# Two graph layers on one core: score rows turned on chip, two softmax passes moved from VectorE to GpSimd

## What is computed

```python
h = relu(layernorm(x))
D = abs(h[:, :, None, :] - h[:, None, :, :])        # 64 x 128 x 128 x 128
t = leaky(batchnorm(einsum('bijc,oc->bijo', D, W1) + b1))   # 64 channels, statistics over b, i, j
s = where(adj > 0, einsum('bijo,uo->bij', t, W2) + b2, -9e15)
A = softmax(s, axis=-1)
y = leaky(batchnorm((A @ h) @ Wg.T + bg))
x = x + concat([h, y]) @ Wt.T + bt
```

## Time and profile before

| | us |
|---|---|
| median of 3 runs | 1188.4 |
| lowest and highest of them | 1184.73, 1188.98 |
| time of the profiled execution | 1189.32 |
| its span, first to last instruction | 1187.5 |
| PE busy | 1062.9 (90%) |
| DVE busy | 1058.1 (89%) |
| ACT busy | 994.8 (84%) |
| POOL busy | 541.3 (46%) |

### The profile page before, as it was taken

How to read it: one execution, slowest core, us unless ns; L and a number is a source line. 1 busy time by engine, 2 the same in 40 slices (tenths; PEclk the granted TensorE clock), 3 DMA queues, 4 the chain that set the end, 5 groups by cost and what they waited for, 6 DMA issues and landing times.

```text
span 1187.5 us, 17527 instructions
## 1 busy us (share of the span) xinstructions
PE 1062.9 (90%) x6376; PEld 463.2 (39%) x6376; DVE 1058.1 (89%) x1418; ACT 994.8 (84%) x1238; POOL 541.3 (46%) x251
## 2 busy tenths in 40 slices
PE   3889999999999999999999599999999999548997
PEld 1333333333333333333333212333333333338886
DVE  6899999999999999999999787999999999435787
ACT  3879999999999899999999599898988989006987
POOL 6466667666666666666667101111122211261331
PEclk9989999999999999999999799999999999758998
DMA  6324343434343334343434789999999998700222
GB/s 165 131 118 177 143 173 146 178 142 164 156 178 142 160 160 177 142 168 152 178 142 188 299 305 358 366 355 360 349 358 350 347 348 296 191 4 12 71 80 72
DMA packets 118005, 237.52 MB, mean 200 GB/s; under 512 B 17568, under 2 KB 65952, under 8 KB 117920
## 3 DMA queue, kind: packets, MB, share of 16 engines
q1 hardware_dynamic: 116336, 235.70, 54.6%
q10 hardware_dynamic: 1584, 0.69, 0.3%
HBM read 126.52 MB, written 109.84 MB: 199 GB/s over the span
## 4 chain that ended last, share of the span: by engine, by line
PE 45%; DVE 32%; ACT 9%; issue 7%; DMA 3%; POOL 2%; SPq 1%; POOLq 0%; DVEq 0%; ACTq 0%
PE psum L708 18%; DVE store L275 12%; PE psum L718 11%; PE psum L722 8%; DVE plain_st L979 4%; ACT store L610 3%; ACT store L556 3%; DVE store L1058 3%; DMA early<-score_rows 2%; PE psum L821 1%; PE psum L680 1%; PE psum L698 1%; PE psum L778 1%; PE psum L855 1%; POOL store L475 1%
## 5 line engine op out<-in xcount | busy, mean ns | idle before, releaser
L708 PE MATMUL psum<-store,w1tt_sb 128*64 128x512 f32 x1792 | 426.0, 605 | 37.4 <-ACT store L556 19.2
L275 POOL TENSOR_TENSOR store<-h_ext 128x2048 f32<-128x2048 f32 (+1 forms) x96 | 386.5, 4028 | 140.9 <-PE psum L708 137.0
L275 DVE TENSOR_TENSOR store<-psum,h_ext 128x2048 f32<-128x2048 f32 x160 | 364.0, 2275 | 0.9 <-ACT h_ext L526 0.9
L556 ACT ACTIVATE store<-store 128x2048 f32<-128x2048 f32 x160 | 305.1, 1929 | 15.2 <-DVE store L275 10.3
L708 PEld LDWEIGHTS psum<-store,w1tt_sb 128*64 128x64 f32 x1792 | 121.7, 137 | 277.5 <-issue 223.5
L610 ACT ACTIVATE store<-store,st 128x1024 f32<-128x1024 f32 x192 | 225.8, 1242 | 1.4 <-DVE st L1045 1.4
L718 PE MATMUL psum<-store,w_twice 128*64 128x512 f32 x768 | 201.5, 603 | 3.9 <-DVE early L944 3.5
L979 DVE BATCH_NORM_STATS2 plain_st<-store 128x6 f32<-128x512 f32 x256 | 160.6, 678 | 0.6 <-ACT store L568 0.6
L722 PE MATMUL psum<-early 128*64 128x512 bf16 x1152 | 158.0, 381 | 0.0
L275 DVE TENSOR_TENSOR store<-h_ext 128x2048 f32<-128x2048 f32 x64 | 139.1, 2173 | 2.6 <-PE psum L708 2.6
L778 PE MATMUL psum<-store,w_rows 128*32 128x512 f32 x1024 | 131.8, 606 | 5.4 <-ACT store L610 5.4
(11 more groups left out here) (153 smaller groups left out, 1143.4 us busy)
## 6 DMA issues: line engine op xcount, KB each, us to landing
kept_products<-store SPq DMA_DIRECT2D x192, 512.0 KB, 2.7
store<-kept_products SPq DMA_DIRECT2D x192, 512.0 KB, 7.5
early<-score_skew SPq DMA_DIRECT2D x16, 384.0 KB, 6.4
early<-adj SPq DMA_DIRECT2D x16, 256.0 KB, 8.0
early<-adj_t SPq DMA_DIRECT2D x16, 256.0 KB, 3.0
store<-x SPq DMA_DIRECT2D x16, 256.0 KB, 4.8
out<-early SPq DMA_DIRECT2D x16, 256.0 KB, 2.4
score_rows<-early SPq DMA_DIRECT2D x64, 32.0 KB, 3.7
```

What stands on the lines that cost most here:

```text
L275: return engine.tensor_tensor(t[:, :, 0:steps, :], nodes.unsqueeze(2).broadcast_to([C, 2, steps, N]), windows(h_ext[:, 2 * c, :], STEP * m ...
L556: nc.scalar.activation(t, t, ACT.Abs).then_inc(abs_ready, 1)
L708: last = nc.tensor.matmul(t[MID * g:MID * g + MID, b, :], w1tt_sb[:, 0:MID], diff[slot][:, g, b * BANK:b * BANK + BANK], start=True, stop= ...
```

## The change

It has these parts:

1. The round trip of the score rows through DRAM is gone (`store_rows`, `load_dist`, `s_dist`). `turn_dist` transposes `s_rows` straight from SBUF in four 128x128 pieces, and `take_turned` sorts the columns in four tensor_tensor instructions, one for each graph.
2. `att_sum` transposes the half matrix only (four PE transposes in place of eight matmuls). The half that isn't transposed is added to the mask on POOL (a second instruction in `sum_half`).
3. The subtraction of the maximum (`shift`) and the product with the reciprocal (`weight`) are POOL instructions. `mask(j + 1)` stands between them.
4. All 16 `x_and_bias` stand behind the last `weight`.
5. `again` computes the last chunk of a couple in full width (`repeats=True`), in one instruction in place of three.
6. All steps are set anew, and the tail has 63 steps in place of 72.

```diff
-        EVAC, DIST_T, TURN, SUM, SCORES, EXP, NORM, TURN_P, COPY, MIX, MIX_COPY, OUT, Y = \
-            19, 32, 33, 50, 52, 56, 58, 61, 62, 64, 65, 67, 69
-        STORE_ROWS, LOAD_DIST, STORE_SKEW, LOAD_HALF, LOAD_ADJ = 21, 26, 35, 41, 30
-        TAIL = 72
+            19, 21, 22, 40, 42, 46, 48, 51, 52, 54, 55, 58, 60
+        STORE_SKEW, LOAD_HALF, LOAD_ADJ = 24, 30, 22
+        TAIL = 63
...
-            if m == PER - 1:
+            if m == PER - 1 and not repeats:
...
             def load_half(j):
                 sp.wait_ge(skew_stored[j % 2], 16 * (j // 2 + 2))
                 if j > 0:
                     sp.wait_ge(s_sum, j)
+                    sp.wait_ge(half_masked, j)
...
                         if j == NQ - 1 and step != LOAD_ADJ:
-                            part = (STORE_ROWS, LOAD_DIST, STORE_SKEW, LOAD_HALF).index(step)
-                            for q in range(4 * part, 4 * part + 4):
+                            for q in range(6) if step == STORE_SKEW else range(6, NQ):
                                 load_x(q)
...
             def sum_half(j):
...
+                pool.wait_ge(half_summed, j + 1)
+                nc.gpsimd.tensor_tensor(mneg[:, :, :], mneg[:, :, :], s_half[:, :, 0:N], ALU.add).then_inc(half_masked, 1)
...
+            def shift(j):
+                pool.wait_ge(max_ready, j + 1)
+                nc.gpsimd.tensor_tensor(s_shift[:, :, :], s_shift[:, :, :], bcast(rows[:, 0, :], N), ALU.subtract)\
+                  .then_inc(s_shifted, 1)
+
+            def weight(j):
+                pool.wait_ge(weight_ready, j + 1)
+                nc.gpsimd.tensor_tensor(prob[:, :, :], prob[:, :, :], bcast(rows[:, 2, :], N), ALU.mult)\
+                  .then_inc(prob_ready, 1)
+
+            mask(0)
             for j in range(NQ):
-                mask(j)
-                if j == NQ - 1:
-                    pool.wait_ge(bt_ready, 1)
-                    for q in range(8):
-                        x_and_bias(q)
                 sum_half(j)
+                shift(j)
+                if j + 1 < NQ:
+                    mask(j + 1)
+                weight(j)
                 if 5 <= j < 5 + MRING:
                     mask_l1(j - 5)
-            for q in range(8, NQ):
+            pool.wait_ge(bt_ready, 1)
+            for q in range(NQ):
                 x_and_bias(q)
...
             def turn_dist(j):
-                pe.wait_ge(dist_in, 16 * (j + 1))
+                pe.wait_ge(rows_ready, j + 1)
                 at_one(QCH * j + DIST_T)
-                for b in range(QUAD):
-                    last = nc.tensor.transpose(att[1].rearrange("p b n -> p (b n)")[:, DIST * b:DIST * b + DIST],
-                                               s_dist[0:DIST, b, :], ident[0:DIST, 0:DIST])
+                for d in range(4):
+                    last = nc.tensor.transpose(att[1][:, d, :], s_rows[:, N * d:N * d + N], ident[:, :])
...
             def att_sum(j):
                 for b in range(QUAD):
-                    nc.tensor.matmul(att[0][:, b, :], ident[:, :], s_half[:, b, 0:N], start=True, stop=False)
-                    last = nc.tensor.matmul(att[0][:, b, :], s_half[:, b, 0:N], ident[:, :], start=False, stop=True)
+                    last = nc.tensor.transpose(att[0][:, b, :], s_half[:, b, 0:N], ident[:, :])
...
             def take_rows(j):
                 if j > 0:
-                    dve.wait_ge(rows_stored, 64 * j)
+                    dve.wait_ge(dist_turned, j)
...
             def take_turned(j):
-                nc.vector.tensor_tensor(s_turn[:, :, :],
-                                        att[1].rearrange("p b n -> p (b n)")[:, 0:QUAD * DIST]
-                                        .rearrange("p (b d) -> p b d", b=QUAD),
-                                        last_mask[:, :].unsqueeze(1).broadcast_to([N, QUAD, DIST]), ALU.mult)\
-                  .then_inc(turn_ready, 1)
+                turned_rows = att[1].rearrange("p d (q m) -> p d q m", q=4)
+                in_order = lambda t: t.rearrange("p (r q d) -> p r q d", r=4, q=4)
+                for b in range(QUAD):
+                    last = nc.vector.tensor_tensor(in_order(s_turn[:, b, :]),
+                                                   turned_rows[:, :, :, 4 * b:4 * b + 4].rearrange("p d q r -> p r q d"),
+                                                   in_order(last_mask[:, :]), ALU.mult)
...
             def att_scores(j):
-                dve.wait_ge(mask_ready, j + 1)
+                dve.wait_ge(half_masked, j + 1)
...
-                linked(nc.vector.tensor_reduce(rows[:, 0, :], s_shift[:, :, :], AX.X, ALU.max))
-                nc.vector.tensor_tensor(s_shift[:, :, :], s_shift[:, :, :], bcast(rows[:, 0, :], N), ALU.subtract)\
-                  .then_inc(s_shifted, 1)
+                nc.vector.tensor_reduce(rows[:, 0, :], s_shift[:, :, :], AX.X, ALU.max).then_inc(max_ready, 1)

             def att_norm(j):
                 linked(nc.vector.tensor_reduce(rows[:, 1, :], prob[:, :, :], AX.X, ALU.add))
-                linked(nc.vector.reciprocal(rows[:, 2, :], rows[:, 1, :]))
-                nc.vector.tensor_tensor(prob[:, :, :], prob[:, :, :], bcast(rows[:, 2, :], N), ALU.mult)\
-                  .then_inc(prob_ready, 1)
+                nc.vector.reciprocal(rows[:, 2, :], rows[:, 1, :]).then_inc(weight_ready, 1)
```

More of the change, by code:

```diff
@@ L146, in two_layers @@
         s_rows = late(0, 512)
-        s_dist = by_graph(late(512, 512))
         s_turn = by_graph(late(1024, 256))
@@ L199, in two_layers @@
             "diff2_ready", "abs2_step", "prod2_ready", "leaky_ready", "scored", "rows_ready"))
-        rows_stored, dist_in, dist_turned, turn_ready, half_in, adj_in, half_summed, mask_ready = (sem(n) for n in (
-            "rows_stored", "dist_in", "dist_turned", "turn_ready", "half_in", "adj_in", "half_summed", "mask_ready"))
+        dist_turned, turn_ready, half_in, adj_in, half_summed, mask_ready = (sem(n) for n in (
+            "dist_turned", "turn_ready", "half_in", "adj_in", "half_summed", "mask_ready"))
         skew_stored = [sem("skew_stored0"), sem("skew_stored1")]
+        max_ready, weight_ready = sem("max_ready"), sem("weight_ready")
+        half_masked = sem("half_masked")
         s_sum, s_masked, dve_att, s_shifted, exp_done, prob_ready, prob_turned, prob_tr_ready, mixed, mix_ready, \
@@ L264, in own, with subtract @@
             return h_ext[:, 2 * c:2 * c + 2, 0:N]
-        def subtract(engine, c, m, slot, op, nodes):
+        def subtract(engine, c, m, slot, op, nodes, repeats=False):
             t = diff[slot].rearrange("p g (d i) -> p g d i", i=N)
             steps = STEP
-            if m == PER - 1:
+            if m == PER - 1 and not repeats:
                 steps = STEP - 1
@@ L337, in load_kept @@
                 sp.dma_start(loaded[k % LRING], kept_dram[k, :, :]).then_inc(kept_in[k % LRING], 16)
-            def store_rows(j):
-                sp.wait_ge(rows_ready, j + 1)
-                for q in range(4):
-                    sp.dma_start(row_dram[j, :, q, :], s_rows[32 * q:32 * q + 16, :]).then_inc(rows_stored, 16)
-            def load_dist(j):
-                sp.wait_ge(rows_stored, 64 * (j + 1))
-                if j > 0:
-                    sp.wait_ge(dist_turned, j)
-                sp.dma_start(s_dist[0:DIST, :, :],
-                             row_dram[j].rearrange("(b r) q (d i) -> (r q d) b i", b=QUAD, i=N)).then_inc(dist_in, 16)
             def store_skew(j):
@@ L393, in _ @@
                           .then_inc(skew_stored[s], 16)
-                for step, do in ((LOAD_ADJ, load_adj), (STORE_ROWS, store_rows), (LOAD_DIST, load_dist),
-                                 (STORE_SKEW, store_skew), (LOAD_HALF, load_half)):
+                for step, do in ((LOAD_ADJ, load_adj), (STORE_SKEW, store_skew), (LOAD_HALF, load_half)):
                     j = quad_at(n - AHEAD, step)
@@ L1053, in again @@
                     dve.wait_ge(prod2_ready, p - 1)
-                subtract(nc.vector, c, m, p % 2, ALU.subtract, own(c)).then_inc(abs2_step, 1)
+                subtract(nc.vector, c, m, p % 2, ALU.subtract, own(c), repeats=True).then_inc(abs2_step, 1)
                 dve.wait_ge(abs2_step, p + 1)
@@ L1069, in take_turned @@
                     dve.wait_ge(skew_stored[(j - 1) % 2], 16 * ((j - 1) // 2 + 2))
[L1070 to L1078 removed]
+                turned_rows = att[1].rearrange("p d (q m) -> p d q m", q=4)
[4 more added lines that the diff above has]
+                                                   in_order(last_mask[:, :]), ALU.mult)
+                last.then_inc(turn_ready, 1)
             links = [0]
```

4 lines of the change are left out of this document (removed).

## The result

The changed kernel takes 1247.2 us (median of 4 runs, 1246.36 to 1250.97) against 1188.7 us for the kernel before (4 runs). The ratio is 1.0501, with a 95% interval of 1.047 to 1.0531: it is 5% slower. The profiled execution took 1246.36 us with a span of 1244.6 us, 57.1 us more than before's 1187.5.

A forecast was written before the change was run, and what follows sets the result against it. DVE set the pace before (21.6 us a quad); a loop over DVE, POOL and PE would set about 25.4. Steady part +48.5, tail -9.4, clock +6: +45 on 1189.3 gives 1234 us, range 1188 to 1258 (narrower 1215 to 1250).

The forecast's parts named there:

- the likeliest one: Both POOL passes wait out a DVE difference and the SCORES-to-SCORES loop sets a period of about 25.4 us; chance 0.59.
- the rival of the clock that falls in every quad: PE's clock drops behind its idle stretch in each quad of the steady part: 1257 us; chance 0.08.
- What bounds the kernel: Steady part before: DVE, busy 258.4 of 264.4 us, sets 21.6 us a quad; relieved of about 1.1, 20.4 by work alone.
- The moved passes: POOL's `shift` and `weight` each wait out L275, end 1.13 us after it and hold the next L1058 by 0.95.
- The loop: From SCORES of one quad to the next, over DVE, POOL and PE: period about 25.4 us in place of 21.6.
- PE standing still from 9.9 to 15.0: In each quad PE reaches TURN_P at about 9.9 us and waits for `weight`, some 5.1 us idle.
- The start: SCORES of quad 0 comes at 726 us, between 725 and 727.3.
- PE's clock: Cost of a lower clock after PE's idleness in each quad: bounds 0 and 29 us in all, a fifth taken, +6.
- The tail: Last `again` to the power: `weight` done at 29.9 us, 16 bias passes 20.3, so 50.2 for 59.6, -9.4 us.
- that POOL is not held up: Rival: POOL's passes do not wait for L275, the loop is 22.4 us, total 1189, no change; chance 0.12.
- the one that had only one pass held: Rival: one of the two POOL passes is held up, or POOL slips ahead: period 23.4 to 24.4, 1203 to 1216 us; chance 0.12.
- The loop does not bind: Faster rival: PE comes to TURN_P late and weights await it, DVE's 20.4 us rules: 1158 us; chance 0.09.

The follow-up runs named there:

- five extra matmuls: Changed kernel with five matmuls of 512 columns, result overwritten, ahead of PE's wait for the weights: 1219.76 us, ratio 1.0244.
- the third order: Changed kernel with other steps only (SUM 42, SCORES 43, NORM 51, TURN_P 55 and on), both passes on POOL: 1193.98 us, ratio 1.0018.

## Why the prediction was right

The forecast was 1234 us, and 1247 came, inside the range of 1188 to 1258 and inside the narrower 1215 to 1250. The case was the likeliest one as to the loop, but together with the rival of the clock that falls in every quad, which I had given a chance of 0.08 and put at 1257 us. By the steps:

- **What bounds the kernel.** Right. The relief of DVE bought nothing, as the period is no longer DVE's work: DVE went from 98% busy to 77%.
- **The moved passes.** Right in kind: both waited out a difference and went ahead of the bit mask. The size was a little too high: 1.04 us for the pass in place of 1.26, an end 0.90 us after the difference instead of 1.13, a hold of 0.72 instead of 0.95. The pass with an operand spread from `rows` is not the bias pass from which I took its time.
- **The loop.** I summed 25.33 us and took 25.4. With the clock kept up it is 24.72 (five extra matmuls). That is -0.7 a period, -8.8 us over 13. The two corrections above, at the places where they enter (0.23 for the end of each pass or hold), make 0.5 of the 0.7.
- **PE standing still from 9.9 to 15.0.** It stood for 4.62 us, to 14.4 us after the start of SCORES. Right.
- **The start.** 723.1 in place of 726: -2.9 us.
- **PE's clock. This is the step that failed**: "5.1 us lies nearest to the row at full speed, so I take a fifth: +6". Measured it is 2.59 us a quad, 33.7 us in all, 27.7 more than taken. Three groups behind the pause make it up: the transposes took 1.12 us for 0.66, the product 3.68 for 1.94 and the scores 1.46 for 1.06 by the timeline, together 2.60. It even exceeds the upper bound of 29, for which I had counted some 4.4 us of work at the lower level, where these took 6. The error was in reading. The four transposes at 1021.71 did run at full speed after 4.34 us of idleness, but the window right behind them, which I had not read, shows the clock lower (columns as in the earlier trace rows):

```profile
1017.40:1021.70 4.30, 0.00 (x0) 0.00 (x0) 4.11 (x7) 0.63 (x1) 1.92 (x1) 1.00 0.76 208
1021.70:1025.90 4.20, 0.66 (x5) 0.43 (x5) 0.69 (x1) 0.00 (x0) 0.53 (x1) 0.63 1.14 261
```

  These are the windows of the kernel before on the two sides of the start of the transposes. Nothing else ran on PE there, so the low clock cost nothing and left no mark in the earlier trace rows. The clock was at 1.00 up to 1022.7 and at 0.50 from 1022.8 on, 0.4 us behind the end of the transposes; PE then stood for another 3.53 us. The run with `weight` on DVE has the same picture with a product behind the transposes, and there the mark is 3.51 us in place of 1.94.
- **The tail.** -12.2 in place of -9.4: `weight` ended 27.9 us after the last `again`, not 29.9, and the 16 bias passes took 19.5 us, not 20.3. That they hold the power is shown: it came 10.2 us earlier with ten of them behind it.
- **The last stage.** I had no term for it, and it came out 1.7 us shorter. In the traces this goes with the clock and not with the change: where the second 10 us behind the power were granted 0.83, as in before, the stage took 121.4 to 121.7 us (four kernels), and where they were granted 1.00, as in after, 119.4 to 119.8 (seven kernels). The three kernels with bias passes behind the power are left out here, as these hold it up. Why the clock rises earlier in the latter is open.

Together, in us, on the +45 of the forecast: clock +27.7, loop -8.8, start -2.9, tail -2.8, last stage -1.7, and 0.6 left over, because the first period was 0.85 us shorter than the others and not 1.45. That is +57.1, the difference of the spans. So the forecast came close partly by luck: a term that was 27.7 us too small met four that were 16.2 too pessimistic together.

The rivals: that POOL is not held up is refuted for this order (2.99 us), and so is the one that had only one pass held. But both are real in other orders: with the steps of before the subtraction took its bare 1.04 us and `weight` 2.99, and in the third order both took 1.04, since DVE goes on with PSUM work there. "The loop does not bind" is refuted by PE's 4.62 us ahead of TURN_P. Its price was not worked out cleanly either: it takes off 15, 9 and 7 us, where its words name 15.6, some 10 for an earlier start and, elsewhere, 9.4 for the tail.

## What to carry to other kernels

Ask of a pass that goes to another engine what that engine will run beside, not how long the pass is: here 0.6 us on DVE became 3.0 on the chain when it met a difference, and 1.04 when it met PSUM work, and of the time that DVE gained most came back as holds of its next instructions (0.72 us behind a pass that had taken 0.61 to 0.69). Before steps are moved closer together, sum the loop from one quad to the next over all engines, since its sum and not the busiest engine's work becomes the period (24.7 us here with the clock kept, against an estimate of 20.4 for DVE's work). And for an engine that will now stand still for some us in each period, look at what its clock does in the windows behind such a pause, with instructions long enough to show it, and over several periods.

## What the runs showed of the hardware

- PE's granted clock fell after pauses of 2.85, 3.57 and 4.62 us that came once in a quad. With 4.62 it did so in every quad, but in the kernel with both passes on DVE it stayed at 1.00 behind two of them, of 3.53 and 2.62 us. After the shorter one and after the 4.34 us in the tail of before, the first 0.66 us of transposes still ran at full speed and the low clock came behind them; after the other two the transposes themselves took 1.1 us. In the changed kernel the low clock covered some 6 us of unbroken work and cost 2.6 us each time; behind the 2.85 us it cost about 1.6. In the kernel before with the passes on POOL, where PE waited 0.95 us for `weight`, the steady part had a clock of 1.00.
- A POOL pass that waited for DVE's difference went ahead of the DVE instruction that stood next, and held it: 0.72 us for the pass of 512 columns, 0.41 for the one of 256.
- POOL's tensor_tensor of 128x512 takes 1.04 us with an operand spread from `rows`, and 1.22 to 1.27 with two full ones or with the bias.
- One-column instructions on DVE took 1.2 us beside POOL's bias passes, against 0.16 where POOL was idle.
